# Two of eight copies of the shift rows moved from ScalarE to VectorE in a fused attention and convolution kernel

## What is computed

```
q, k, v = W x + b                       # 8 rows each for q and k, per image
attn    = softmax(q^T k, axis=-1)       # 256 x 256 per image
layer 0:  x = gamma * (Wo (v attn^T) + bo) + x
layer 1:  x = x + v attn^T
layer 2:  batch norm, 3x3 convolution, batch norm, 3x3 convolution, shortcut (1-bit weights)
layer 3:  whitening by a 4x4 Cholesky factor per channel group, a linear map, a bias
```

## Time and profile before

| | us |
|---|---|
| median of three executions | 69.20 |
| the profiled execution, its own time | 69.05 |
| span of the profiled execution, first to last instruction | 67.3 |
| around the span (69.05 - 67.3) | 1.75 |
| TensorE busy | 57.7 |
| VectorE busy | 48.0 |
| ScalarE busy | 42.5 |
| GpSimd busy | 20.0 |

### The profile page before, as it was taken

One profiled execution on the slowest core, in us unless ns is written; L12 is line 12 of the kernel. 1 busy time (PEld: TensorE's weight loads), 2 busy tenths in 40 slices (PEclk: granted clock), 3 DMA queues, 4 the chain that ended last, 5 costly groups with the idle time before them and its releaser, 6 DMA issues. The chain is left out here.

```text
span 67.3 us, 2133 instructions
## 1 busy us (share of the span) xinstructions
PE 57.7 (86%) x795; PEld 36.7 (54%) x795; DVE 48.0 (71%) x133; ACT 42.5 (63%) x137; POOL 20.0 (30%) x58
## 2 busy tenths in 40 slices
PE   5994898889899989958998989999499999999910
PEld 3323433655465627432553758698385997855500
DVE  0079899595949899994946775988949978575530
ACT  0711098999997699789998663930028564167630
POOL 5000955530554608680303040301303050045000
PEclk9999999999999999999999999999999999999999
DMA  0998930000000000000000000000000000000044
GB/s 0 254 245 205 370 151 0 0 0 10 0 0 5 0 0 0 0 19 0 0 0 0 0 0 10 0 0 10 0 0 0 10 0 0 10 0 0 0 166 146
DMA packets 2457, 2.71 MB, mean 40 GB/s; under 512 B 400, under 2 KB 2064, under 8 KB 2448
## 3 DMA queue, kind: packets, MB, share of 16 engines
q1 hardware_dynamic: 2160, 2.39, 11.5%
q10 hardware_dynamic: 288, 0.20, 0.9%
HBM read 2.06 MB, written 0.52 MB: 38 GB/s over the span
## 5 line engine op out<-in xcount | busy, mean ns | idle before, releaser
L507 ACT ACTIVATE bank<-bank,negmax 128x256 f32<-128x256 f32 x32 | 14.5, 457 | 1.7 <-DVE negmax L1054 1.7
L683 PE MATMUL bank<-const-bfloat16-1.0 128*64 128x512 bf16 x82 | 11.5, 418 | 0.8 <-PEq L1362 0.8
L1054 DVE TENSOR_REDUCE negmax<-bank 128x2 f32<-128x512 f32 x16 | 10.5, 685 | 1.9 <-PE bank L742 1.8
L527 ACT ACTIVATE probs<-bank 128x512 f32<-128x512 f32 x16 | 8.8, 602 | 1.1 <-PE bank L766 1.1
L805 PE MATMUL bank<-probs,vt 128*64 128x256 f32 x64 | 8.5, 386 | 0.3 <-DVE cut L1064 0.3
L910 PE MATMUL bank<-hi,taps 64*64 64x225 f16 (+2 forms) x144 | 6.9, 267 | 0.1
L683 PEld LDWEIGHTS bank<-const-bfloat16-1.0 128*64 128x64 bf16 x82 | 4.7, 117 | 4.2 <-issue 1.6
L507 ACT ACTIVATION_READ_ACCUMULATOR bank<-bank,negmax 128x1 f32 x32 | 6.9, 216 | 0.0
L910 PE MATMUL bank<-lo,taps 64*64 64x225 f16 (+2 forms) x144 | 6.9, 266 | 0.0
L360 POOL TENSOR_TENSOR cut<-cut 64x256 f32<-64x256 f32 x7 | 4.3, 610 | 8.3 <-DVE cut L1064 5.3
L910 PEld LDWEIGHTS bank<-hi,taps 64*64 64x64 bf16 x144 | 5.8, 107 | 0.9 <-issue 0.4
(11 more groups left out here) (134 smaller groups left out, 103.3 us busy)
## 6 DMA issues: line engine op xcount, KB each, us to landing
cw<-conv_w SPq DMA_DIRECT2D x2, 288.0 KB, 4.2
x<-x_in SPq DMA_DIRECT2D x4, 128.0 KB, 2.6
out<-res SPq DMA_DIRECT2D x4, 128.0 KB, 1.8
kst<-consts SPq DMA_DIRECT2D x1, 428.0 KB, 4.9
aw<-attn_w ACTq DMA_DIRECT2D x1, 128.0 KB, 2.5
aw<-attn_w SPq DMA_DIRECT2D x1, 128.0 KB, 3.0
half<-select SPq DMA_DIRECT2D x1, 96.0 KB, 2.7
kst<-consts SPq DMA_DIRECT2D x1, 64.5 KB, 3.4
```

Of the source, the lines that this page charges most:

```text
L507: nc.scalar.activation(part, part, ACT.Exp, bias=negmax[:, i % 2, n:n + 1], accum_out=total[:, i % 2, n:n + 1]).then_inc(total_out, 1)
L527: nc.scalar.activation(probs[:, i % 2, g], pb_t[g][:].rearrange("p (t n) -> p t n", t=CH), ACT.Exp).then_inc(exp_out, 1)
L683: mm(bank[lanes(h)], filler[:, lanes(h)], filled, start=True, stop=True)
L1054: ve.tensor_reduce(negmax[:, i % 2, g * CH:(g + 1) * CH], pb_s[(2 * i + g) % 3][:].rearrange("p (t n) -> p t n", t=CH), AX.X, ALU.max, neg ...
```

## The change

The copies of the rows of i = 5 and i = 6 leave ScalarE's program and enter VectorE's. VectorE's `shift_rows` waits for the same semaphore values and raises the same one. The copy of i = 5 stands between maxima(6, 1) and queries_keys(7), the last cast; the copy of i = 6 stands between add_shortcut(4) and statistics(0). The copies of the other six pairs stay where they are. Nothing else is moved, and no byte moved by a DMA changes.

```diff
@@ ScalarE's program
             shift_rows(4)
             exps(4)
             totals(6, 0)
-            shift_rows(5)
             totals(6, 1)
             exps(5, range(0, 1))
             logs(6)
             exps(5, range(1, 2))
             totals(7, 0)
-            shift_rows(6)
             totals(7, 1)
             logs(7)
             exps(6)
@@ VectorE's program
+            def shift_rows(i):
+
+                dve.wait_ge(rows_mm, i + 1)
+                dve.wait_ge(t_mm, 2 * (i - 1))
+                ve.tensor_copy(shift_t[:, i % 2, :], pb_rows).then_inc(rows_out, 1)
+
...
             maxima(6, 0)
             values_out(5)
             maxima(6, 1)
+            shift_rows(5)
             queries_keys(7)
             maxima(7, 0)
             maxima(7, 1)
             add_shortcut(4)
+            shift_rows(6)
             statistics(0)
             values_out(6)
             add_shortcut(5)
```

## The result

| | before | after |
|---|---|---|
| executions of the first comparison, us | 69.11 to 69.22, and two of 70.42 and 70.53 | 68.75, 68.76, 68.92, and three of 70.25 to 70.29 |
| the profiled execution, its own time | 69.05 | 68.75 |
| its span | 67.3 | 67.0 |

The changed kernel takes 0.9948 of the time of before, with a 95% interval of 0.9927 to 0.9968: about 0.36 us faster, where 0.34 were forecast. Some executions of both kernels are 1.2 to 1.5 us longer than the others, so this ratio and all that follow compare the shorter executions only, and the plain median of the changed kernel, 69.59 us, says nothing of the change.

The account below looks back on a forecast made before the run. ScalarE's queue was taken to set the end of the attention; 0.06 (copy of i = 5) + 0.28 (copy of i = 6) = 0.34 us, so 69.20 - 0.34 = 68.86 us, range 68.72 to 69.10.

Parts of the forecast that it names:

- the release by the last maxima: ScalarE's totals(7, 0) can start 0.04 after the first of these maxima ends, so of 0.27 only 0.06 us survives.
- The cover of 0.1: VectorE's 0.49 us gap ahead of the last cast hides the copy of i = 5 by about 0.1 us.
- Rival C: VectorE's queue becomes the bound ahead of the last cast: slower, 69.59 us; chance 0.05.
- The slack of 0.03: TensorE can start shifts_to_rows(7) at 35.96, GpSimd releases it at 35.99: 0.03 us to spare.
- rival B: TensorE holds the gain through a later add_shifts(6): gain 0.10, time 69.10 us; chance 0.15.
- The place where last_shortcut lets go: On TensorE, shifts_to_rows(6) can start there, between 33.27 and 33.47 us.
- the low end of the range: Largest gain TensorE's own list allows, 0.37, with unknown overlaps of up to 0.1 us on top: 68.72 us.
- Rival A: ScalarE gets the copies' whole durations back; TensorE follows only by 0.37 us, time 68.83 us; chance 0.06.
- Rival D: VectorE is late at the stage's end, values_out(7) delaying mix(7): gain 0.20, time 69.00 us; chance 0.05.

Follow-up runs that it names:

- e1: Changed kernel with VectorE's copy of i = 6 taken out, so only the copy of i = 5 moves: ratio to before 0.9989.
- e5: Changed kernel with totals' wait for shift_out removed, leaving its wait for max_out: ratio to before 0.9930, profiled 69.04 us.
- f2: Changed kernel with weight_sum(1) moved between the copy of i = 5 and the last cast, second run: ratio to before 1.0025.
- e3: Changed kernel with statistics(0) in front of VectorE's copy of i = 6 instead of behind it: ratio to before 1.0036.
- e2: Changed kernel with VectorE's copy of i = 5 taken out, so only the copy of i = 6 moves: ratio to before 0.9970.
- f3: Changed kernel, weight_sum(0) moved behind statistics(0), VectorE doing the first of GpSimd's two splitting subtractions for pair 7, second run: ratio to before 0.9932.
- e8: Kernel before, with weight_sum(0) moved and the first splitting subtraction of pair 7 given to VectorE: ratio to before 1.0133 (0.9948 to 1.0318).

## Why the prediction was right

**The time.** 0.36 us were measured where 0.34 were forecast, and that this is so close is partly luck. The interval of the ratio allows 0.22 to 0.51 us. The traces say 0.31, and there an error of 0.05 in one direction and one of 0.02 in the other partly cancel. The forecast of 68.86 us also adds the 0.15 us by which the median before lay above its profiled execution; the changed kernel took 68.75, 68.76 and 68.92 us, and 68.75 in its profiled execution, so this distance was not there again.

**The bound, and ScalarE's queue.** Right. The copy of i = 6 was to be worth 0.28 and the copy of i = 5 0.06. From totals(7, 0) to logs(7) the changed kernel takes 34.87 - 32.90 = 1.97 us against 35.18 - 32.91 = 2.27: 0.30 for the copy of i = 6, 0.02 more than its distance of 0.28 in the earlier trace rows. The forecast read ScalarE's list as one without a gap, but this copy had waited 0.03 to 0.04 for its rows (e1), and that wait went with it.

**The first copy, mis-sized.** In its place of 0.06 stands 0.01. The step that failed is the release by the last maxima: I took 0.04 from the end of a maximum to the exponential, but totals(7, 0) began 0.10 after 32.80. The row is of an iteration that waits for one semaphore, this one for two, and with the second taken away e5 had the 0.04 again. With 0.10 for the release the kernel before was already at its limit there: 32.80 + 0.10 = 32.90 against 32.91. The sum is 0.31 instead of 0.34.

**VectorE's costs.** Right: 0.41 against the 0.42 of the cast of the same shape, starts at 30.31 and 33.72 against 30.34 and 33.76, the last cast still at 30.88. The cover of 0.1 measured 0.16. Rival C's mechanism is real: in f2 the last cast was 0.42 late and so was everything behind it. But the copy alone held nothing up.

**TensorE.** Right in kind: add_shifts(6) at 34.19 against 34.24, shifts_to_rows(7) at 36.02 against 35.99. The slack of 0.03 that I gave rival B was too small. It is 0.16 (e3): add_shifts(6) came 0.05 and mix(5) 0.06 earlier than forecast, mix(5) lets its follower go after 0.87, not 0.91, and GpSimd released shifts_to_rows(7) 0.03 later. The place where last_shortcut lets go is 33.29 by the forecast's own sum (33.47 - 0.18), not 33.27, and shifts_to_rows(6) did start at 33.29. In the same way the low end of the range comes out at 68.73, not 68.72; nothing hangs on either.

**Rival A and the rule on open latency.** If the copies had given back their whole durations, exps(5) would have moved by 0.40 and the copy of i = 6 would have been worth 0.38. exps(5) moved by 0.27 and logs(6) by 0.26, and the copy of i = 6 gave 0.30, its wait for the rows included. So a copy of 128x256 on ScalarE hides 0.10 to 0.13 us under the next instruction (0.38 - 0.28 and 0.40 - 0.27). The Trainium skill's rule in "Advanced Engine Details and Errata", section "The Read-Write Bubble", is that instructions are not pipelined into each other on ScalarE and VectorE. The trace does not agree with it as rival A applies it, to the durations in the profile; the measurement decides.

**The end of the stage.** Right: values_out(7) started at 37.83, in time for mix(7), since add_shortcut(6) and all behind it kept the 0.31 us; from shifts_to_rows(7) to the end of the span it was 67.3 - 36.33 = 30.97 us before and 67.0 - 36.02 = 30.98 after. Rival D did not occur.

## What to carry to other kernels

An item moved off a full queue was worth its distance to the next item there, not its duration, and only as far as the next thing that the queue has to wait for: the two copies here were equal, and alone one was worth 0.26 us at the end of the stage (e2) and the other 0.04 (e1). Where it is put counts as much: the receiving queue needs an idle gap at that point, and the same copy placed behind two small statistics instructions instead of in front of them turned 0.31 us of gain into 0.20 of loss. A change that frees one engine makes the next one visible: here in turn ScalarE's wait for the maxima, then VectorE's queue in front of the last cast and TensorE's own list.

## What was not expected

- With a wait for two semaphores ScalarE started 0.10 us after the end of what released it; with one of the two taken away it was 0.04 (e5).
- Where ScalarE had hardly a wait between exps(5) and logs(7), its logarithm followed the last activation by 0.64 us, elsewhere by 0.60 (e2). What makes the difference is open.
- GpSimd's shifts(6) took 0.08 to 0.09 us longer in the kernels where VectorE does a subtraction for pair 7, though its three instructions lasted 0.20 each as always: in f3 the second started 0.37 behind the first, where 0.28 is the distance of before (32.97 - 32.69). It cost e8 its 0.10. What holds it is open. The rows of f3:

```profile
32.55 0.20 POOL L376 TENSOR_TENSOR shift<-negmax,lntot 128x4 f32<-128x4 f32 x1 [2.69 <-issue]
32.92 0.20 POOL L380 TENSOR_TENSOR shift<-shift 128x4 f32<-128x4 f32 x1 [0.17 <-POOL shift L376]
33.20 0.20 POOL L383 TENSOR_TENSOR shift<-shift 128x4 f32<-128x4 f32 x1
```
